# Stage 1 of a two-layer graph network: the max scan runs on the shifted relu, and epsilon enters with the exponential

## The reference, cut to what matters

```
m = node_feats[src] + (edge_feats @ We + be)
m = relu(m) + EPS                                   # EPS = 1e-7
zmax = segment_max(m, dst)
ez = exp(m - zmax[dst])
denom = segment_sum(ez, dst)
agg = segment_sum(m * ez / denom[dst], dst)
feats = node_feats + agg
out = feats @ Wm + bm
```

## Time and profile before

| | before |
|---|---|
| median of three runs | 2280.22 us (2271.97 to 2284.08) |
| profiled execution | 2278.03 us, span 2276.2 us |
| POOL busy | 1622.1 us (71%) |
| PE busy | 1250.3 us (55%) |
| DVE busy | 1198.0 us (53%) |
| ACT busy | 725.9 us (32%) |
| stage 1, 1177 to 2189 us: POOL busy | 761.95 us in 784 instructions |
| stage 1: DVE busy, ACT busy | 549.11 us, 443.37 us |
| stage 1: DMA share, granted TensorE clock | 0.42, 0.62 of full speed |

### The profile page before, as it was taken

One profiled execution on the slowest core, in us unless ns is written; L12 is line 12 of the kernel. 1 busy time (PEld: TensorE's weight loads), 2 busy tenths in 40 slices (PEclk: granted clock), 3 DMA queues, 4 the chain that ended last, 5 costly groups with the idle time before them and its releaser, 6 DMA issues.

```text
span 2276.2 us, 18899 instructions
## 1 busy us (share of the span) xinstructions
PE 1250.3 (55%) x4739; PEld 908.2 (40%) x4739; DVE 1198.0 (53%) x2001; ACT 725.9 (32%) x1383; POOL 1622.1 (71%) x1683
## 2 busy tenths in 40 slices
PE   5208877777778777777503444344334434444435
PEld 4106655555555555556402222233222323232224
DVE  4106755555555555555534555555556555555556
ACT  3002322222222222222214444444444444444431
POOL 3577777777777777777367777777777777777743
PEclk9958978778787778877756656665566566666655
DMA  9845645555555555555323444444444444444431
GB/s 293 284 155 162 195 148 151 145 155 143 154 153 142 156 152 151 149 147 149 85 47 102 120 109 118 111 119 114 112 114 121 109 121 107 120 109 113 115 91 40
DMA packets 200307, 306.14 MB, mean 134 GB/s; under 512 B 66407, under 2 KB 109306, under 8 KB 200071
## 3 DMA queue, kind: packets, MB, share of 16 engines
q1 hardware_dynamic: 94928, 129.97, 18.6%
q0 software_dynamic: 53840, 83.74, 16.6%
q10 hardware_dynamic: 51432, 91.24, 12.0%
HBM read 183.72 MB, written 121.03 MB: 134 GB/s over the span
## 4 chain that ended last, share of the span: by engine, by line
POOL 68%; issue 22%; PE 3%; DMA 3%; DVE 2%; SPq 2%; ACT 0%; ACTq 0%; POOLq 0%; DVEq 0%
POOL rows L423 33%; POOL block L416 23%; POOL rows L416 8%; PE bank L595 2%; POOL typed L445 1%; DMA d_inj<-zeros 1%; POOL d_inj L436 1%; SPq L333 1%; PE wide L712 1%; POOL H L460 1%; DMA w_nodes<-in_b 1%; DVE typed L750 0%; PE wide L710 0%; SPq L300 0%; SPq L305 0%
## 5 line engine op out<-in xcount | busy, mean ns | idle before, releaser
L423 POOL DMA_INDIRECT rows<-d_x,idx x784 | 762.2, 972 | 258.2 <-issue 249.1
L416 POOL DMA_INDIRECT block<-d_h,idx x576 | 553.1, 960 | 175.6 <-issue 175.6
L673 PE MATMUL bank<-ident,rows 128*128 128x128 f32 x392 | 109.3, 434 | 630.5 <-DMA rows<-d_x,idx 630.5
L673 PEld LDWEIGHTS bank<-ident,rows 128*128 128x128 f32 x392 | 70.2, 217 | 766.2 <-DMA rows<-d_x,idx 766.2
L917 DVE TENSOR_TENSOR_SCAN block<-keep,block,h3d 128x512 f32<-128x512 bf16 x98 | 126.8, 1294 | 464.1 <-ACT h3d L540 464.1
L416 POOL DMA_INDIRECT rows<-d_h,idx x208 | 198.7, 955 | 78.5 <-issue 63.1
L814 DVE TENSOR_SCALAR score<-bank 128x8 f32<-128x8 f32 x98 | 16.3, 166 | 398.5 <-PE bank L638 398.5
L638 PEld LDWEIGHTS bank<-half_sum,prod 128*128 128x128 f32 x784 | 191.0, 328 | 1.8 <-DVE prod L840 1.8
L682 PE MATMUL wide<-ident,block 128*128 128x128 f32 x784 | 187.7, 421 | 6.4 <-DVE block L939 6.4
L638 PE MATMUL bank<-half_sum,prod 128*128 128x2 f32 x784 | 186.4, 359 | 1.6 <-DVE prod L840 1.6
L537 ACT ACTIVATE prod<-bank 128x512 f32<-128x512 f32 x98 | 58.5, 597 | 387.6 <-PE bank L673 387.6
(11 more groups left out here) (154 smaller groups left out, 2327.3 us busy)
## 6 DMA issues: line engine op xcount, KB each, us to landing
d_run<-block ACTq DMA_DIRECT2D x98, 512.0 KB, 2.8
d_inj<-zeros SPq DMA_DIRECT2D x28, 896.0 KB, 17.0
inj<-d_inj SPq DMA_DIRECT2D x98, 256.0 KB, 3.8
d_run<-stage ACTq DMA_DIRECT2D x98, 256.0 KB, 3.2
feat<-in_ea16x3T SPq DMA_DIRECT2D x196, 96.0 KB
types<-d_type SPq DMA_DIRECT2D x196, 64.0 KB
keep<-d_keep SPq DMA_DIRECT2D x196, 64.0 KB
feat<-in_ea32T SPq DMA_DIRECT2D x196, 64.0 KB, 1.9
```

The costliest lines, as they stand in the source:

```text
L416: pool.indirect_dma_start(out=ring[c % RING][:, j % TILES, j // TILES, :], out_offset=None, in_=d_h24, in_offset=bass.IndirectOffsetOnAxis ...
L423: pool.indirect_dma_start(out=rows1[c % 2][:, j % TILES, j // TILES, :], out_offset=None, in_=d_x1, in_offset=bass.IndirectOffsetOnAxis(ap ...
L673: ins = pe.matmul(p_m[s][:, j:CH:TILES], rows1[s][:, j, :, :].rearrange("p h c -> p (h c)"), ident[:, :], is_transpose=True, start=False, ...
```

## The change

The scan now runs on `relu` with one column in front, which holds the last value of the chunk before. It takes the maximum first and adds the penalty second, so that its output at an edge is already the masked maximum in front of that edge. The separate addition of the penalty (L921) goes, and so does the ScalarE instruction that made `m` (L540). The epsilon, which cancels in `y`, is added in the product (a `scalar_tensor_tensor` in the place of a `tensor_tensor`). The column copy remains but now reads the other slot's `relu` and has to stand behind this chunk's `relu`, since both write the same tile. Since `before` is the maximum in front of an edge, the maximum at the cut between the halves needs the edge's own value too: two stores of 128 KB for each chunk instead of one, two small gathers at the end instead of one, and one more small maximum.

```diff
-        relu, m, y, down, mexp = prod, h3d, q2_sb, msg, run
+        before, y, down, mexp = h3d, q2_sb, msg, run
...
-        runmax = [carve(CH + 1) for s in range(2)]
+        relu = [carve(CH + 1) for s in range(2)]
...
             def load_pen(s, r, of_edge):
                 sp.wait_ge(s_lists, 48)
-                wait(sp, shift_ready[s], r)
+                wait(sp, before_ready[s], r)
...
             def messages(s, r, c):
                 act.wait_ge(z_ready[s], r + 1)
-                act.activation(relu[s][:, :], p_m[s][:, :], ACT.Relu).then_inc(relu_ready[s], 1)
-                act.wait_ge(relu_ready[s], r + 1)
                 wait(act, mexp_ready[s], r)
-                act.activation(m[s][:, :], relu[s][:, :], ACT.Copy, bias=EPS).then_inc(m_ready[s], 1)
+                wait(act, max_out[s], 32 * r)
+                act.activation(relu[s][:, 1:CH + 1], p_m[s][:, :], ACT.Relu).then_inc(relu_ready[s], 1)
...
             def store_max(s, r, c):
-                act.dma_start(d_max.rearrange("(c e) a -> c (e a)", c=C)[:, bass.ds(c * CH, CH)],
-                              runmax[s][C:P, 1:CH + 1]).then_inc(max_out[s], 16)
+                for of_edge, values in ((d_before, before[s][C:P, :]), (d_own, relu[s][C:P, 1:CH + 1])):
+                    act.dma_start(of_edge.rearrange("(c e) a -> c (e a)", c=C)[:, bass.ds(c * CH, CH)],
+                                  values).then_inc(max_out[s], 16)
...
-                then(dve.memset(runmax[s][:, :], 0.0))
+                dve.memset(before[s][:, :], 0.0)
+                then(dve.memset(relu[s][:, 0:1], 0.0))
...
             def maxima(s, r, c):
-                first = c == 0
-                wait(dve, max_out[s], 16 * r)
-                if not first:
-                    dve.wait_ge(max_ready[1 - s], 2 * (r + s))
-                dve.tensor_copy(runmax[s][:, 0:1], runmax[1 - s][:, CH:CH + 1]).then_inc(max_ready[s], 1)
+                dve.wait_ge(relu_ready[s], r + 1)
+                wait(dve, max_out[s], 32 * r)
+                if c > 0:
+                    dve.tensor_copy(relu[s][:, 0:1], relu[1 - s][:, CH:CH + 1]).then_inc(carried[s], 1)
+                    dve.wait_ge(carried[s], r + s)
+                    dve.wait_ge(before_ready[1 - s], r + s)
                 dve.wait_ge(pen_in[s], 32 * (r + 1))
-                dve.wait_ge(m_ready[s], r + 1)
-                dve.tensor_tensor_scan(runmax[s][:, 1:CH + 1], keep[s][:, :], m[s][:, :], runmax[1 - s][:, CH:CH + 1],
-                                       ALU.add, ALU.max).then_inc(max_ready[s], 1)
-                dve.wait_ge(max_ready[s], 2 * r + 2)
+                dve.tensor_tensor_scan(before[s][:, :], relu[s][:, 0:CH], keep[s][:, :], before[1 - s][:, CH - 1:CH],
+                                       ALU.max, ALU.add).then_inc(before_ready[s], 1)
+                dve.wait_ge(before_ready[s], r + 1)
                 wait(dve, updown_ready[s], 2 * r)
-                dve.tensor_tensor(y[s][:, :], runmax[s][:, 0:CH], keep[s][:, :], ALU.add).then_inc(shift_ready[s], 1)
-                dve.wait_ge(shift_ready[s], r + 1)
-                dve.tensor_tensor(y[s][:, :], m[s][:, :], y[s][:, :], ALU.subtract).then_inc(y_ready[s], 1)
+                dve.tensor_tensor(y[s][:, :], relu[s][:, 1:CH + 1], before[s][:, :], ALU.subtract).then_inc(y_ready[s], 1)
...
-                dve.tensor_tensor(mexp[s][:, :], m[s][:, :], expm[s][:, :], ALU.mult).then_inc(mexp_ready[s], 1)
+                dve.scalar_tensor_tensor(mexp[s][:, :], relu[s][:, 1:CH + 1], EPS, expm[s][:, :],
+                                         ALU.add, ALU.mult).then_inc(mexp_ready[s], 1)
```

More of the change, by code:

```diff
@@ L84, in gnn_program @@
         d_run1 = scratch("d_run1", [EP, 2 * C])
-        d_max = scratch("d_max", [C * HALF, 1])
+        d_before = scratch("d_before", [C * HALF, 1])
+        d_own = scratch("d_own", [C * HALF, 1])
         ident = sb("ident", [P, P])
@@ L135, in gnn_program @@
         mb_i = sb("mb_i", [C, 1], i32)
-        max_ab = sb("max_ab", [C, 2])
+        max_ab = sb("max_ab", [C, 3])
         max_ab_wide = sb("max_ab_wide", [C, 2, NP])
@@ L231, in gnn_program @@
         got1_rows, feat1_in, pen_in = sems("got1_rows"), sems("feat1_in"), sems("pen_in")
-        z_ready, relu_ready, m_ready = sems("z_ready"), sems("relu_ready"), sems("m_ready")
-        max_ready = sems("max_ready")
-        shift_ready, y_ready = sems("shift_ready"), sems("y_ready")
+        z_ready, relu_ready = sems("z_ready"), sems("relu_ready")
+        carried, before_ready, y_ready = sems("carried"), sems("before_ready"), sems("y_ready")
         updown_ready, decay_ready, expm_ready = sems("updown_ready"), sems("decay_ready"), sems("expm_ready")
@@ L453, in _ @@
             for s in range(2):
-                pool.wait_ge(max_out[s], 16 * (CHUNKS // 2))
-            pool.indirect_dma_start(out=max_ab[:, 1:2], out_offset=None, in_=d_max,
-                                    in_offset=bass.IndirectOffsetOnAxis(ap=mb_i[:, 0:1], axis=0)).then_inc(s_mb, 16)
+                pool.wait_ge(max_out[s], 32 * (CHUNKS // 2))
+            for q, of_edge in ((1, d_before), (2, d_own)):
+                pool.indirect_dma_start(out=max_ab[:, q:q + 1], out_offset=None, in_=of_edge,
+                                        in_offset=bass.IndirectOffsetOnAxis(ap=mb_i[:, 0:1], axis=0)).then_inc(s_mb, 16)
             for s in range(2):
@@ L947, in _ @@
             steps(step1, 0, 1)
-            dve.wait_ge(s_mb, 16)
-            then(dve.tensor_copy(max_ab[:, 0:1], runmax[1][0:C, CH:CH + 1]))
-            dve.tensor_copy(max_ab_wide[:, :, :], max_ab[:, :].unsqueeze(2).to_broadcast([C, 2, NP])).then_inc(s_maxwide, 1)
+            dve.wait_ge(s_mb, 32)
+            then(dve.tensor_tensor(max_ab[:, 0:1], before[1][0:C, CH - 1:CH], relu[1][0:C, CH:CH + 1], ALU.max))
+            then(dve.tensor_tensor(max_ab[:, 1:2], max_ab[:, 1:2], max_ab[:, 2:3], ALU.max))
+            dve.tensor_copy(max_ab_wide[:, :, :], max_ab[:, 0:2].unsqueeze(2).to_broadcast([C, 2, NP])).then_inc(s_maxwide, 1)
             dve.wait_ge(s_maxps, 1)
```

## The result

The changed kernel takes 2321.28 us (median of four runs, 2320.04 to 2322.63) where the kernel before, now with a fourth run, took 2279.89 us (2271.97 to 2284.08): a ratio of 1.0186 with a 95% interval of 1.0157 to 1.0214. It is slower by 41 us; 2325 us were predicted.

The account below looks back on a forecast made before the run. GpSimd's gathers bound the loop: 69 to 75 us of new stretching, taken as 70, less 22 gone, gave +46 us, ends -1: 2323 us profiled, 2325 us median. Range for 8 in 10: 2303 to 2350 us.

Parts of the forecast that it names:

- The bound: Stage 1 loop: L423's gathers, 762.2 us, plus 249.1 us "issue" set its length; ScalarE and VectorE work is worth nothing.
- The phase of the scan: Each chunk's scan starts 0.49 us earlier, 0.27 us behind the relu's end and about 0.50 us ahead of the fourth gather.
- The fourth gather: In each of 91 chunks the scan catches the fourth gather, which lasts 1.54 us, 0.60 us more.
- The fifth gather: The product catches each chunk's fifth gather, which lasts 1.08 to 1.14 us, 0.14 to 0.20 us more.
- What goes: The loop's present stretching of gathers, 22 us, disappears, since its places are the same two or three gathers.
- The shifted chunks: Six chunks with a GpSimd pause: scan about 1 us ahead of the third gather, 0.12 + 0.14 us, 2 us in all.
- The second store: 98 more DMAs of 128 KB on ScalarE's queue: taken as 0, bounds -10 and +10 us through the landing.
- The ends: Ahead of the loop 0, bounds -1 and +1; behind it -1.2 us from VectorE's shorter last chunk.
- The sum: Loop +46 us and ends -1 give +45 us on the profiled 2278.03 us: 2323 us, 2325 us for the median.
- Rival A: The change is off the path and only the tail counts: 2279 us, chance 0.08.
- Rival B: The scan starts behind the fourth gather and escapes, 10 us of stretching left instead of 22: 2267 us, chance 0.06.
- Rival C: Same mechanism at the fourth gather, scan nearer the edge at -0.2 to -0.3 us: 2342 to 2356 us, chance 0.1.

Follow-up runs that it names:

- the epsilon alone: Kernel before with only the epsilon moved into the product, old scan, L921 and one store kept: 2325.63 us, ratio 1.0189; on a slow chip 2670.88 us.
- the scan alone: Changed kernel with m made by ScalarE again and the shifted scan run on it, both stores kept: 2280.35 us, ratio 0.9993; on a slow chip 2668.98 us.
- the memset of 256 columns: Changed kernel with an idle 128x256 VectorE memset in front of the copy in every chunk: 2349.67 us, ratio 1.0291; on a slow chip 2684.3 us.

## Why the prediction was right, step by step

- *The bound.* Right. The loop grew by 41.6 us, and L423's busy time by 41.6 us; "issue" stayed at 249.1. ScalarE is 61.4 us less busy (62 forecast) and VectorE 57.3, a little less than the 60 to 68 forecast; neither shows in the chain.
- *The phase of the scan.* 0.49 us earlier was forecast, 0.53 us measured (median -0.014 before, -0.547 after, over the 91 ordinary chunks). The relu-to-scan gap is 0.22 us in the median, not 0.27: the copy starts 0.03 us behind the relu (1611.61 to 1611.64), not 0.10, and takes 0.15 us, not 0.126. The 0.10 us was read from a scan behind ScalarE and doesn't hold for a copy; a scan behind ScalarE shows it again with the epsilon alone (1604.42 to 1604.52).
- *The fourth gather.* 0.60 us forecast from the earlier trace rows; 0.54 us measured (median 1.49), which is the 0.05 us of phase. Over 91 chunks this makes the loop's forecast some 5 us too high.
- *The fifth gather.* 0.14 to 0.20 us forecast, 0.145 measured (median 1.089); the product lasts 0.685 us, so the 0.75 us of the stage-0 instruction didn't carry over.
- *What goes.* The 22 us went, as forecast, but not for the reason given. The largest part, 9.7 us, lay on the sixth gather and not on the same two or three that are stretched now; it went because the subtraction and the product come earlier and meet the fifth instead.
- *The shifted chunks.* 0.12 + 0.14 us forecast; 0.05 us on the third gather and 0.14 us on the fourth measured.
- *The second store.* Nothing. The landing of a chunk's last gather, from its start to TensorE's, has a median of 2.46 us before and 2.47 after, and of 2.48 us both with the epsilon alone (one store) and with the scan alone (two stores), which ran on one chip.
- *The ends.* Wrong in sign, by a little. Ahead of the loop 0 was forecast and 1.9 us came, of which 1.4 before the layer norm's gathers and 0.5 in them; the change touches little there, and why they came is not shown. Behind the loop -1.2 us was forecast and +0.8 measured: VectorE's last chunk is 1.26 us shorter (8.76 us from the relu's start at 2237.43 to the last scan's end at 2246.19, 10.02 before), but the last gathers landed 0.4 us later and GpSimd's pause of 2 us, which recurs every 112 gathers, now falls in front of the first L461 instead of behind it, since one small gather more stands ahead, so that this gather meets a VectorE instruction and lasts 2.27 us.
- *The sum.* That the profiled execution, 2322.63 us, hits the 2323 of the sum is partly luck: the loop was forecast at +46 us and grew by 41.6, the ends at -1 and came to +2.7. The medians of the runs lie 41.4 us apart where 45 were forecast.

The timeline rows of the gather behind the loop:

```profile
2254.89 1.83 DVE L963 TENSOR_TENSOR late<-wgt,cross 125x1600 f32<-125x1600 f32 x1 [2.59 <-DMA cut<-d_run]
2255.27 2.27 POOL L461 DMA_INDIRECT H<-d_run,last_i  x1 [7.55 <-issue]
```

The Trainium skill (SBUF - State Buffer, section "Who interferes with whom") calls the port that VectorE and GpSimd share an exclusive lock on which the later one "fully blocks", and names two SBUF inputs against a GpSimd instruction that reads SBUF. The traces agree: a gather caught by such an instruction waits for its end, to within 0.03 us. They add that the gather is exposed only at its start, and that it holds nothing up itself, for the changed kernel's scan starts inside a gather 97 times and always lasts 1.28 us. The section's inference that a tensor_tensor leaves descriptor generation alone is not borne out: 96 gathers besides the one at 1605.19 had started inside L923, and all were stretched.

Rival A (off the path) is refuted by the result. Rival B (escape) is real as a mechanism, seen in the run of the scan alone, but the changed kernel was 0.45 us on the other side of it (-0.55 against the edge at -0.10). Rival C was reached by the memset of 256 columns: 2349.67 us, inside its 2342 to 2356 (the kernel before took 2283.12 us beside it).

## What to carry to other kernels

Where GpSimd's indirect DMAs set the pace, look at what VectorE runs at each gather's start, not at how busy it is: an instruction with two SBUF inputs costs the gather that it catches up to 1.0 us here (a 128x512 scan), one with an input in PSUM nothing. Less work on an idle engine can cost time by moving such an instruction over a start, so reckon the phase before shortening a chain. Taking the second input from PSUM removed the sensitivity to phase altogether, here for 0.7% below the kernel before and, by the two ratios to it, 2.5% below the changed one.

## What the runs showed of the hardware that I had not expected

- A gather is exposed for an instant only. A two-input instruction that started 0.099 us or more ahead of its recorded start and is still running makes it wait for the end; one that starts 0.096 us ahead or later costs nothing, even if it covers all of the gather (one exception in 7840).
- On two chips the same programs took 2670 to 2690 us, with stops of 5 to 17 us of single engines (ScalarE for 17.07 us until 1916.10) whose releaser the profile doesn't name, and a change worth 41 us elsewhere was worth nothing there (1.0008). Two kernels can only be compared beside each other on one chip.
- In stage 1 of the six traces taken where the kernel before takes 2280 us, GpSimd pauses six times, for 1.94 to 2.23 us and 112 gathers apart; in stage 0, with as many gathers, it never does. What it does then is not shown.
